# A decoder of two layers on one core: all stretches behind the set-up joined to one, and a 0/1 matrix made by ScalarE

## The reference

```python
x = x + latent_attention(ln(x))                 # 16 heads of 16, keys and values through 64 latent channels
x = x + cross_attention_over_heads(ln(x), ctx)  # softmax over the 16 heads of one token, head size 64
x = x + mixture_of_depths(ln(x))
x = x + sparse_attention(ln(x))                 # each row keeps its 25 largest scores
x = x + masked_cross_attention(ln(x), ctx)      # keys behind a given length are off
x = x + ternary_linear(ln(x))

def mixture_of_depths(h):                       # h: 256 tokens x 256
    scores = h @ w_router
    top, idx = top_k(scores, 128)               # the 128 tokens with the highest scores
    sel = h[idx]
    y = gelu(sel @ W1 + b1) @ W2 + b2
    return h.at[idx].add(sigmoid(top)[:, None] * y)
```

## Time and profile before

| what | us |
|---|---|
| three runs | 6017.2, 6035.1, 6035.79 (median 6035.1) |
| the profiled execution, device time | 6033.22 |
| its span, first to last instruction | 6031.4 |
| TensorE busy in it | 5402.1 (90%) |
| VectorE busy | 4518.6 (75%) |
| ScalarE busy | 3706.0 (61%) |
| GpSimd busy | 2307.4 (38%) |

### The profile page before, as it was taken

One profiled execution on the slowest core, in us unless ns is written; L12 is line 12 of the kernel. 1 busy time (PEld: TensorE's weight loads), 2 busy tenths in 40 slices (PEclk: granted clock), 3 DMA queues, 4 the chain that ended last, 5 costly groups with the idle time before them and its releaser, 6 DMA issues. The chain is left out here.

```text
span 6031.4 us, 113615 instructions
## 1 busy us (share of the span) xinstructions
PE 5402.1 (90%) x39450; PEld 3816.4 (63%) x39450; DVE 4518.6 (75%) x16189; ACT 3706.0 (61%) x9249; POOL 2307.4 (38%) x4100
## 2 busy tenths in 40 slices
PE   7899999899898999899998898989999899999987
PEld 4666666666666666566666666666666666666654
DVE  2477887777887777787777887777887777887774
ACT  3466676666676666666665666656666666676542
POOL 0233443334443334443333443334443334443341
PEclk7799999999999999999999999999999999998876
DMA  2000000000000000000000000000000000000000
GB/s 88 4 5 7 8 8 6 7 8 5 8 7 10 5 8 5 9 8 8 5 8 7 7 8 8 5 7 6 8 8 6 7 8 6 7 7 8 3 5 6
DMA packets 29387, 53.44 MB, mean 9 GB/s; under 512 B 8145, under 2 KB 9810, under 8 KB 27986
## 3 DMA queue, kind: packets, MB, share of 16 engines
q1 hardware_dynamic: 28770, 45.73, 2.5%
HBM read 37.33 MB, written 8.39 MB: 8 GB/s over the span
## 5 line engine op out<-in xcount | busy, mean ns | idle before, releaser
L1044 DVE MATCH_REPLACE8 wk<-m,wk 128x256 f32<-128x256 f32 x2048 | 835.9, 423 | 0.0
L1065 POOL TENSOR_SCALAR mx<-m 128x2 f32<-128x2 f32 x512 | 114.3, 223 | 1761.2 <-DVE wk L1044 1755.9
L479 DVE TENSOR_REDUCE m_nm<-bankM 128x2 f32<-128x512 f32 x1024 | 656.4, 692 | 168.6 <-PE bankM L469 166.4
L1040 DVE MAX8 m<-wk 128x8 f32<-128x256 f32 x2048 | 772.0, 425 | 0.0
L1074 POOL TENSOR_TENSOR t_pr<-wk,sc 128x256 f32<-128x256 f32 x1024 | 738.1, 741 | 3.8 <-issue 1.4
L1077 POOL TENSOR_TENSOR t_pr<-t_pr,sc 128x256 f32<-128x256 f32 x1024 | 728.4, 732 | 0.0
L810 ACT ACTIVATE xk_area<-bankH,xb 64x256 f32<-64x256 f32 x1024 | 479.8, 469 | 296.3 <-PE bankH L712 278.1
L1001 ACT ACTIVATE t_pr<-t_pr,t_nm 128x256 f32<-128x256 f32 x1024 | 475.9, 510 | 153.8 <-POOL t_pr L1077 141.5
L528 PE MATMUL bankM<-m_q,m_kT 32*128 32x512 f32 x2048 | 565.1, 631 | 0.0
L469 PE MATMUL bankM<-m_kT,m_q 32*128 32x256 f32 x4096 | 535.6, 399 | 10.3 <-DVE m_nm L479 8.9
L570 PE MATMUL bankT<-ident,t_pr 128*128 128x128 f32 x2048 | 342.9, 292 | 120.1 <-ACT t_pr L1001 117.7
(11 more groups left out here) (223 smaller groups left out, 11926.7 us busy)
## 6 DMA issues: line engine op xcount, KB each, us to landing
xin<-x_in SPq DMA_DIRECT2D x32, 256.0 KB, 2.6
ctxA<-ctx_in SPq DMA_DIRECT2D x32, 256.0 KB, 2.6
ctxB<-ctx_in SPq DMA_DIRECT2D x32, 256.0 KB, 2.8
out<-x SPq DMA_DIRECT2D x32, 256.0 KB, 2.0
w<-w_w SPq DMA_DIRECT2D x2, 1024.0 KB
xwq<-w_xwq SPq DMA_DIRECT2D x1, 1024.0 KB
xwk<-w_xwk SPq DMA_DIRECT2D x1, 1024.0 KB
xwv<-w_xwv SPq DMA_DIRECT2D x1, 1024.0 KB
```

The lines of the kernel that those rows point to most:

```text
L479: nc.vector.tensor_reduce(b["nm"][:, i % 2, 2 * (i // 2) + x, :], banks[u % 4][:].rearrange("p (j s) -> p j s", j=2), AX.X, ALU.max, negat ...
L1040: link.inc(nc.vector.max(top, src[:, t, :]))
L1044: m = nc.vector.match_replace(out=wk[:, k, t, :], in_to_replace=take, in_values=src[:, t, :], imm_value=-BIG)
```

## The change

All stretches behind `start` become one, without a loop: `passes("all", ...)` is written once, with `m` for 31 sequences, `h`, `t` and `c` for 32. The order tables are put in a row: `whole` takes the letters of `ORDER_FIRST`, of `ORDER` seven times and of `ORDER_LAST`, after leaving out those beyond the number of chunks that the streams have (`CHUNKS`). The fillers are put in a row in the same manner. The second edit moves the 0/1 matrix from VectorE to ScalarE: `Square(rank - slot)`, twice, then `Relu(1 - that)`, twice, with two new semaphores; the order tables lose two `h` for each pass on VectorE and gain one on ScalarE, as in these two lines of the loop's table for VectorE.

```diff
-        h2 t4 c t2 m2 h m2 h m2 t m4 t m3 t m2 t m t4 h t2 h2 t2 h t5 h t2 c h6 m h2 m2 t2 m t2 h3 c t c t2 c h c t2 h c3 m c t c2 t2 c3 t c
+        t4 c t2 m2 h m2 h m2 t m4 t m3 t m2 t m t4 h t2 h2 t2 h t5 h t2 c h4 m h2 m2 t2 m t2 h3 c t c t2 c h c t2 h c3 m c t c2 t2 c3 t c t4 c6
...
+CHUNKS = {"pe": dict(h=57, t=39, c=34, m=33),
+          "act": dict(h=86, t=82, c=26, m=26),
+          "dve": dict(h=32, t=73, c=29, m=24),
+          "pool": dict(h=15, t=52, c=7, m=4)}
+
+
+def whole(order, chunks, **laps):
+
+    left, kept = {k: chunks[k] * n for k, n in laps.items()}, []
+    for letter in order:
+        if left.get(letter):
+            left[letter] -= 1
+            kept.append(letter)
+    return "".join(kept) + "".join(k * n for k, n in left.items())
+
+
+ORDER_ALL = {e: whole(ORDER_FIRST[e], n, m=2, h=2, t=1) + whole(ORDER[e], n, m=LAPS, h=LAPS, t=LAPS, c=LAPS) * ((B - 4) // LAPS)
+             + whole(ORDER_LAST[e], n, h=2, t=3, c=4, m=1) for e, n in CHUNKS.items()}
+
+
+def filler_rows(letter):
+
+    return FILL_FIRST.get(letter, []) + FILL[letter] * ((B - 4) // LAPS) + FILL_LAST[letter]
+
+
+FILLERS = {letter: filler_rows(letter) for letter in FILL}
...
-            table = {"loop": FILL, "first": FILL_FIRST, "last": FILL_LAST}.get(lap["of"], {})
-            if letter in table:
-                for _ in range(int(table[letter][lap["n"] - first[letter]][place])):
+            if lap["of"] == "all":
+                for _ in range(int(FILLERS[letter][lap["n"] - first[letter]][place])):
...
-            pe.wait_ge(*at(g["md_e"], 6))
+            pe.wait_ge(*at(g["md_pick"], 2))
...
+            act.wait_ge(*at(g["md_e"], 4))
+            for t in range(NT):
+                nc.scalar.activation(pick[:, t, :], w["iota"][:, 0:CAP], ACT.Square, bias=rank[:, t:t + 1], scale=-1.0).then_inc(g["md_off"], 1)
+            for t in range(NT):
+                act.wait_ge(*at(g["md_off"], 1 + t))
+                nc.scalar.activation(pick[:, t, :], pick[:, t, :], ACT.Relu, bias=ones[:, 0:1], scale=-1.0).then_inc(g["md_pick"], 1)
+            yield
...
-            for t in range(NT):
-                yield
-                dve.wait_ge(*at(g["md_e"], 3 + t))
-                nc.vector.tensor_scalar(pick[:, t, :], w["iota"][:, 0:CAP], rank[:, t:t + 1], None, ALU.is_equal).then_inc(g["md_e"], 1)
...
-            dve.wait_ge(*at(g["md_e"], 7))
+            dve.wait_ge(*at(g["md_e"], 5))
...
-            dve.wait_ge(*at(g["md_e"], 8))
+            dve.wait_ge(*at(g["md_e"], 6))
...
-            order = {"start": ORDER_START, "first": ORDER_FIRST, "last": ORDER_LAST, "loop": ORDER}[lap["of"]]
+            order = {"start": ORDER_START, "all": ORDER_ALL}[lap["of"]]
...
-        loops = (nb - 3) // LAPS
-        rest = nb - loops * LAPS
         passes("start", m=(0, 0, 0))
-        passes("first", m=(1, 0, 1), h=(0, 0, 1), t=(0, 1, 1))
-        with nc.Fori(0, (loops - 1) * LAPS + 1, LAPS) as i:
-            passes("loop", m=(i + 3, 0, LAPS - 1), h=(i + 2, 0, LAPS - 1), t=(i + 1, 0, LAPS - 1), c=(i, 0, LAPS - 1))
-        spans = dict(h=(nb - rest + 2, 0, rest - 3), t=(nb - rest + 1, 0, rest - 2), c=(nb - rest, 0, rest - 1))
-        if rest > 3:
-            spans["m"] = (nb - rest + 3, 0, rest - 4)
-        passes("last", **spans)
+        passes("all", m=(1, 0, nb - 2), h=(0, 0, nb - 1), t=(0, 1, nb), c=(0, 2, nb + 1))
```

More of the change, by code:

```diff
@@ new lines @@
+        c2 t c m h c h2 m2 t c h t h2 t m c m h c h2 t m2 h t m t h m t m h m c m h t h2 m h2 m t m2 t m2 t m2 h m h m t m t h t h2 m t m2 h3 t
+        h t h4 m h2 m2 h c h t m t m h t m t c2 t h3 c h2 t c h3 t2 h2 t h2 c t h t h t c h t c3 t h c t h t2 h2 c t c h4 c2 t h t c t c h c t
+        c2 h t2 h2 t h c2 t h3 t c2 t c h t h c h t h c2 h c t h t h c t c t h t h t c2 h c t h2 t h8 c h c t c t c t c t c t c2 t3 c t2 c t2 c
+        t2 c t c t c t2 c2 t c5 t c t2 c3 t c2 t c t2 c t c2 t4 c3 t3 c t5 c32"""),
@@ new lines @@
+    "act": runs("""
+        h c h3 c t c h t4 m t2 h2 t2 h2 t2 h4 c t2 h3 c h t h t h t3 h t h t h2 t h t2 h4 t3 h2 t h t h3 t3 c h4 c t2 c2 t2 c t c t h4 t c3 t3 h
+        c t c t c t2 c2 t h t h3 c2 h t c t h c t c h4 t h t c m t2 m h m h2 t h3 t h t m2 h2 c t h3 t h t4 h3 t h2 t h t h c t2 h2 t3 h m h t
+        m2 t m t m t2 m2 t m t m h t m h m h t2 m h2 m2 h t h m t h m4 h t h c h t5 m c h t h2 t2 c h t c h t h3 t h t h2 t h t h t2 h t h2 t h2
+        t3 h4 t2 h t3 h2 t h2 t3 h4 t2 h2 t h t h t2 h4 t3 h c t h5 t2 c h c t h5 t c t c t2 c2 h t c2 h t4 h2 t h2 c t h c t h3 t2 h2 t2 h c2
+        t2 c h3 t h2 t c h c t2 h t h t c2 t h t c t h t h t3 c t4 h t h c h3 t h c h c h t c3 t31 c t4 c2 t2 c2 t3 c t2 c3 t2 c t c2 t c2 t c
+        t2 c t4 c2 t2 c t3 c t12 c t6 c t4 c2 t c23"""),
@@ L99 @@
[L99 removed]
+        c2 t c h t2 h2 t h m t12 c m t3 m h t11 h t4 h t3 h c3 h t4 h t h2 t m t5 h t h t c t2 h t2 c2 h t h t h t12 h t6 h c t3 h t3 h t3 h t6
+        h t3 h t3 h t h t8 h3 c5 t c t20 c t21 c2 t c t8 c t c6"""),
 }
@@ new lines @@
+        c t c h3 c t m h2 t h t2 c h2 m c m2 t h m2 t h2 m t m2 t h2 m h m t h m h m t m t m t m4 t m3 c h t m h t m3 t m2 h m h t m h t m t m
+        h4 t h4 t h c t h3 c t h t c t c2 t m c h2 c2 h t h2 c2 h t h2 c h t h c t h c t h c2 h t c h t c h c2 t c h t c2 h2 c2 t h2 c3 t h2 c t
+        h c t h2 c t h c h2 t h m t c t c h2 m2 t m h m2 h2 t m t m h2 m t m h2 m2 t h t m t m t m2 t m3 h m3 t m t h m3 t m h m2 h t m h t m t
+        m h4 t h4 t h c h t h2 c t h c t c t c h c2 t c h t h c h2 c h t h c h c h t h t c t c h2 c h c t c h c h c t c t c t h c2 h t h c2 h c2
@@ new lines @@
+        h c m h2 t c h t c t c h2 c t m h3 t h t2 c h2 m c m2 t h m2 t h m h t m h t m h m h m h t m h m t m t m t m5 t c m2 h t m h t m3 t m h
+        m2 h t m h t m t m h4 t h4 t h c h3 c t2 h t c t c2 m t c2 h2 c h2 t h c2 h t h2 c h t h c t h c t h c h c t c h t c h c2 t c h c t c h2
+        c2 t h c3 t h3 c t h c t h c h t h c h2 t h m t c t c h2 m2 t m h m2 h2 m t m h t h m t m h2 m2 t h t m t m t m2 t m4 h m2 t m t h m3 t
+        m h m2 h t m h t m t m h6 t h2 t h"""),
+    "act": runs("""
+        h2 c h t c h c h t h c t2 h t2 c h t5 h t h2 t h3 m t h2 t2 h t h2 t h t h2 t c2 h2 c t2 h2 t c2 h t h t2 c h2 t c2 t h2 t h2 c t c2 h t
+        h3 t c3 h4 t c h t h2 c t h3 c t c h t c h2 t h3 t h t c t h4 t h t3 h m t h2 t h3 t c h t h t h3 m4 t4 h2 t2 h t h t h t h2 t4 m t m t
+        m2 t m2 t m t c m2 t4 m2 t h m3 h t3 m2 t m2 h t h2 t m t h t m h t h2 c h c t h t h t c t3 h t3 c h t h t h7 t3 h2 t2 h3 t2 h t h2 c t
+        h2 t c2 h t h c2 t h2 t c t c t m t h2 t c h4 t c3 h4 t2 c3 h2 t h2 c t3 h t c h5 c2 h t c h t h4 t3 h c h5 t4 h t h m h t h c h3 t m t2
+        h m h m t m t h3 t2 h t2 h3 t3 h2 t5 m t m t m t2 m4 t2 m2 t2 m2 t h m3 t h t2 m2 t m h m t h2 m t2 h t m h t h c h2 t h c h2 c t h t c
+        t4 h c h t4 h t h2 t h3 t h t h3 t m t h t h t h2 t c2 h t h t h2 c t c2 t h t c h t h2 t c2 t h2 t h2 c t c t c h4 t c3 h4 t2 c h c h2
+        t h3 c t c h t c h t h4 t c h t2 h4 t h t3 h m t h2 t h3 t c t h2 t h2 m4 t3 h t h2 t h t h t h t h t h t4 m t m2 t c m2 t m2 t2 m2 t4
+        m2 h t m3 h t3 m2 t m2 t h3 t m t h t m h t h2 t h c h2 t h c t c t2 h t2 c h t3 h t h6 t3 h t h4 t3 h t h c t h3 c2 t h t h c2 t h2 t3
+        c m c t h2 t c h4 t c3 h4 t c t c2 h2 t h2 c t4 c h6 c2 h t c h t h4 t h t2 c h5 t4 h t h m t c h4 t h t2 m h2 m2 t m t h t h3 t h t2 h2
+        t h t h t6 m t m t2 m t m4 t2 m2 t2 m2 t h m3 h t3 m h m t m t m h2 m t2 h t m h t h"""),
@@ L136 @@
+        t h t h m t3 h t2 h c2 t h c t7 h2 t4 m t3 h2 t2 c t h t6 c t2 h t m t h c h t3 h t3 c t9 h t3 h m h t3 m t2 h t c t c t h t2 h c t4 h2
+        t2 m t2 c t3 h2 m t9 h c2 t2 h t h t h t6 c t2 h t7 h t2 m t h t3 m h t h t2 c3 t2 h t4 h2 t h t5 m t3 h2 t3 h t6"""),
 }
```

78 lines of the change are left out of this document (23 added, 55 removed).

## The result

The changed kernel took 5949.65 us (median of four runs, 5922.4 to 5959.65), the kernel before, on the same chip, 6030.02 us (four runs, 6017.2 to 6035.79). The ratio is 0.9862, with a 95% interval of 0.9823 to 0.9902: some 80 us less. The forecast was 5989 us, with a range from 5965 to 6012; the direction was right, and the gain was nearly twice the 44 us that were forecast.

What follows compares the result with a forecast made beforehand. TensorE, busy 90% of the span, was taken as the bound, with its stops and half-clock stretches. From 6033.2 us, minus 47.2 for the joining, plus 3 for the moved matrix: 5989 us, range 5965 to 6012.

Steps and rivals of the forecast that it cites:

- the first term of the sum: At the loop's six jumps back: each costs 5.43 us more than a straight entry, 32.6 us in all.
- It isn't made up later in the turn: After a jump, the 5.97 us lost in the first pass stays lost: first turn 717.64 us, six others 723.07 each.
- The straight entries: At eight entries with drain and barrier but no jump: TensorE's 1.82 us gap each, 14.6 us saved by joining.
- The joining as a whole: Removing jumps and straight entries between stretches: 32.6 + 14.6 = 47.2 us saved, at least 39.5, upper end 58.4.
- The moved matrix: Before the gather: 1.42 us in place of 1.39, nothing in 28 passes; slower in four quiet passes, +3 us.
- Barriers partly free: At stretch ends: VectorE's shorter gap counts, half the slower clock comes back; gain 33.5, 6003 us; chance 0.13.
- Stalls of the fetch in the straight list: In TensorE's long straight list: fetch stalls or clock drops elsewhere take two thirds of the gain; 6018 us; chance 0.07.
- A slower gather: At the gather: unoverlapped activations add 1.1 us a pass, longer half clock 1.7 us in 28; 6069 us; chance 0.04.
- Faster still: Joining gives 58 us, activations take 1.16 us: 5974 us, or lower if half-clock stretches go; chance 0.10.
- The signs: Trace marks of a right forecast, at projections, former stretch ends and gather, including turns of 716 us or less.
- VectorE's idle time behind the count: Sign at VectorE's wait for TensorE after the second count: over 9 us, from 7.75 us behind the comparisons before.

Runs made afterwards that it cites:

- the written-out loop: The kernel before with its hardware loop written out, all nine stretches and their barriers kept, matrix on VectorE: 5964.19 us, 0.9916 of before.
- the joining alone: The kernel before with one stretch in place of nine, without barriers, matrix left to VectorE: 5963.27 us, 0.9904 of before.
- the first four kernels: Runs beside before (6013.3 us): joining only 5963.27, matrix moved only 6030.64, loop written out 5964.19, changed kernel again 5944.18 us.
- the experiment with one activation more: The changed kernel with one unused activation before the squares, gather 0.29 us later in a middle pass: 5986.86 us, 0.9929 of before.

## Why the prediction was wrong

**The step that failed** is the first term of the sum: "six jumps cost 6 x 5.43 = 32.6 us more than straight entries, and this is measured on whole turns, with all that overlaps". Measured by the written-out loop, it is 49 us (51 by the turns of the profiles), 8 us a jump. The mechanism was right (TensorE stands still for 5.9 us behind a jump, then gets half a clock); the size was taken from one turn without a jump, and that turn was not a clean one. Its pass 1 had a half-clock stretch of 6.8 us and a short one that most turns of the written-out loop escape, and so 4.5 us of what a turn behind a jump carries stood on both sides of the subtraction and fell out. "It isn't made up later in the turn" was the right question, put to one sample only. Behind this stands a premise of the whole sum: each stop was given its own length and the slower clock right behind it, and the clock of all other passes was taken to stay as it was. The two terms below failed by that too.

**The straight entries**, 8 x 1.82 = 14.6 us, were found in pass 0, and dearer than forecast: 3.3 us each, with the half clock that follows. They came to 1 us in the time of the joining alone (5963.3 against 5964.2 us; 7 us by the ratios), since pass 1 gave them back. With the moved matrix behind it, the same joining keeps them (710.0 us a turn), and they are worth 32 to 41 us. The joining as a whole, 50 us by itself for a forecast of 47.2, looks right, but that is luck: the jumps were taken too low by as much as the entries were too high.

**The moved matrix** was right by its rows: 1.36 us from count to gather for a forecast of 1.42, and 0.9 us more in the quiet passes. As a term of the sum it was wrong by its context: about +11 us by itself with the jumps (forecast +3), -19 us in the joined kernel. A difference of hundredths of a microsecond at the gather can't give -19 us by itself. What the profiles show is that more turns have the pattern of 710.0 in place of 713.4, by the one stretch shown above (six and four of seven in the two profiles of the changed kernel, one of seven in that of the joining alone); that is 10 to 18 us. Why the moved matrix does this is open.

**Sum by what was measured**: 49 for the jumps, 1 for the barriers, 19 for the matrix in this place, 69 us in the runs of the first four kernels (6013.3 to 5944.2); 80 us in the first comparison. Forecast 44. In this order of the edits the matrix is the term that is off by most (-19 for +3). In the other order, by the ratios, the matrix comes first with +11, then the jumps with some -53 and the barriers with -32 to -41. The terms don't add up independently, so no split of the gain is the only one.

**The rivals.** Barriers partly free (6003 us): true of the joining alone, but beside a jump that was dearer. Stalls of the fetch in the straight list (6018): not found; no entry without a releaser stands before the projections. A slower gather (6069): not found by itself, but the experiment with one activation more shows that its second half, a delay that costs clock, can happen at 0.3 us already: 6.8 us a turn, of which only 1.2 are the delay. Faster still (5974, "or lower if a few of the half-clock stretches ... go too"): this is what happened, in pass 1 and not behind the gather, where the clock is still 0.51 (0.52 before). At 0.10 it was given too little, and the range ended at 5965 because the lower end took only the stretches that I could name.

**The signs.** Turns of 716 us or less, no gap behind L820 and, at the place shown, a clock of 1.00, 1.3 to 1.5 us to the gather: all seen. VectorE's idle time behind the count was to be over 9 us; it was 8.57 in the middle pass, 7.28 at the same place before, so it grew by 1.3 us and stayed under 9. The sign was taken from another pass, with 7.75 us. The row of the changed kernel, then that of before (L614 is L639):

```profile
2131.57 0.37 DVE L639 RECIPROCAL m_rd<-bankM 128x16 f32<-128x16 f32 x2 [8.57 <-PE bankM L630]
...
2184.30 0.37 DVE L614 RECIPROCAL m_rd<-bankM 128x16 f32<-128x16 f32 x2 [7.28 <-PE bankM L605]
```

## What to carry to other kernels

A pass taken as a yardstick must itself be looked at by its granted clock: compare the clock of every pass of the turn, not only the sum, before two turns are subtracted. Where a schedule repeats and its clock moves between two levels, the price of a stall is its own length plus the half-clock stretches that it brings or takes away, here up to a pass later, and the range should be as wide as one such stretch in every turn, on both sides. Even with a body of 720 us this hardware loop was worth writing out, since the engine that bounds the kernel stood still at the jump.
